# Where the third down product is added, which quarter of weights starts the groups of seven, and which engine rounds the sums of the weights

## The reference, cut to what matters

```python
x = x + tanh(g_ffn[0]) * ffn(layernorm(x))
# ffn: x is (2048, 256); Wg, Wu are (8, 256, 1024), Wd is (8, 1024, 256)
for wg, wu, wd in zip(Wg, Wu, Wd):
    h = silu(x @ wg) * (x @ wu)
    acc = acc + h @ wd
```

## Time and profile before

| | |
|---|---|
| median of 3 runs | 1277.64 us (1277.58 to 1279.3) |
| profiled execution: time, span of its instructions | 1277.64 us, 1275.6 us |
| PE busy (matmuls) | 1242.6 us, 97% |
| PEld busy | 987.7 us, 77% |
| DVE busy | 1105.9 us, 87% |
| POOL busy | 968.8 us, 76% |
| ACT busy | 691.4 us, 54% |
| granted TensorE clock | 0.995 |
| mean DMA rate | 38 GB/s |

### The profile page before, as it was taken

One profiled execution on the slowest core, in us unless ns is written; L12 is line 12 of the kernel. 1 busy time (PEld: TensorE's weight loads), 2 busy tenths in 40 slices (PEclk: granted clock), 3 DMA queues, 4 the chain that ended last, 5 costly groups with the idle time before them and its releaser, 6 DMA issues.

```text
span 1275.6 us, 18422 instructions
## 1 busy us (share of the span) xinstructions
PE 1242.6 (97%) x6149; PEld 987.7 (77%) x6149; DVE 1105.9 (87%) x1779; ACT 691.4 (54%) x1456; POOL 968.8 (76%) x901
## 2 busy tenths in 40 slices
PE   7999999999999999999999999999999999999998
PEld 5778777777777777777777777777777777787775
DVE  5987799999999999999999999999999974677546
ACT  2455455555555555555555555555555545545543
POOL 3635898899989999888998888899989725444435
PEclk9999999999999999999999999999999999999999
DMA  4020200001100000000000000001100330000121
GB/s 136 26 91 1 92 25 26 25 26 41 34 26 25 25 26 25 25 26 25 25 26 25 26 26 25 25 25 39 37 25 1 116 116 1 18 22 14 35 96 62
DMA packets 42365, 48.27 MB, mean 38 GB/s; under 512 B 4239, under 2 KB 40143, under 8 KB 42015
## 3 DMA queue, kind: packets, MB, share of 16 engines
q1 hardware_dynamic: 38720, 43.07, 10.3%
q0 software_dynamic: 1440, 3.41, 0.7%
q10 hardware_dynamic: 2111, 0.63, 0.2%
HBM read 37.36 MB, written 10.29 MB: 37 GB/s over the span
## 4 chain that ended last, share of the span: by engine, by line
PE 66%; DVE 17%; ACT 9%; issue 5%; POOL 2%; DMA 0%; ACTq 0%; POOLq 0%; DVEq 0%
PE bank L1270 18%; PE bank L1271 17%; PE bank L1272 17%; DVE hid_lo L1929 4%; DVE acc L1958 3%; ACT PC L1013 2%; PE bank L1508 2%; PE bank L1517 2%; DVE m_accM L1958 1%; DVE t_loT L1929 1%; ACT hid_hi L953 1%; DVE half_g L1894 1%; ACT half_g L929 1%; PE bank L1670 1%; DVE hid L1904 1%
## 5 line engine op out<-in xcount | busy, mean ns | idle before, releaser
L1270 PE MATMUL bank<-xop_hi,w_hi 128*128 128x512 f32 x896 | 352.4, 393 | 3.3 <-ACT half_g L929 2.3
L1271 PE MATMUL bank<-xop_lo,w_hi 128*128 128x512 f32 x896 | 351.8, 393 | 0.0
L1272 PE MATMUL bank<-xop_hi,w_lo 128*128 128x512 f32 x896 | 351.3, 392 | 0.0
L1921 DVE TENSOR_TENSOR hid_lo<-hid,hid_hi 128x512 fp32r<-128x512 f32 x227 | 261.0, 1182 | 3.8 <-ACT hid_hi L953 3.7
L1270 PEld LDWEIGHTS bank<-xop_hi,w_hi 128*128 128x128 f32 x896 | 168.4, 188 | 45.2 <-ACT half_g L929 3.0
L1272 PEld LDWEIGHTS bank<-xop_hi,w_lo 128*128 128x128 f32 x896 | 168.3, 188 | 38.2
L1271 PEld LDWEIGHTS bank<-xop_lo,w_hi 128*128 128x128 f32 x896 | 168.5, 188 | 37.9
L953 ACT CAST hid_hi<-hid 128x512 fp32r<-128x512 f32 x227 | 140.1, 621 | 62.3 <-PE bank L1272 48.3
L937 ACT ACTIVATE s<-bank 128x512 f32<-128x512 f32 x128 | 78.3, 612 | 109.2 <-PE bank L1272 109.2
L1270 PE MATMUL bank<-hid_hi,wd_hi 128*128 128x512 f32 x338 | 134.4, 398 | 1.4 <-DVE hid_lo L1921 1.4
L1271 PE MATMUL bank<-hid_lo,wd_hi 128*128 128x512 f32 x338 | 133.9, 396 | 0.0
(11 more groups left out here) (272 smaller groups left out, 2648.5 us busy)
## 6 DMA issues: line engine op xcount, KB each, us to landing
raw_gu<-in_L_ffn_Wg_dram SPq DMA_DIRECT2D x32, 256.0 KB, 2.7
raw_gu<-in_L_ffn_Wu_dram SPq DMA_DIRECT2D x32, 256.0 KB, 3.1
raw_d<-in_L_ffn_Wd_dram SPq DMA_DIRECT2D x32, 256.0 KB, 3.6
slots<-empty_row SPq DMA_DIRECT2D x1, 2080.0 KB, 10.0
xr<-slots SPq DMA_DIRECT2D x8, 260.0 KB, 4.8
x_res<-in_x_dram SPq DMA_DIRECT2D x4, 512.0 KB, 5.2
x_mid<-x_res SPq DMA_DIRECT2D x1, 2048.0 KB, 9.0
x_res<-x_mid SPq DMA_DIRECT2D x4, 512.0 KB, 5.6
```

Source lines behind the costliest of these rows:

```text
L1270: mm(ps, w, a, start=start, stop=False, skip_group_check=True)
L1271: mm(ps, w, a_low, start=False, stop=False, skip_group_check=True)
L1272: return mm(ps, w_low, a, start=False, stop=True, skip_group_check=True)
L1921: nc.vector.tensor_tensor(out=hid_lo[n % 2][h][:], in0=hid[h][:], in1=hid_hi[n % 2][h][:].bitcast(F32), op=ALU.subtract).then_inc(lo_ready ...
```

## The change

1. `FIRST_SEVEN = 3`: the groups of seven begin with quarter 3, not 2, so there are 28. The conditions of SP's loads and of the first `split_down_sums` move with it.
2. `group_behind_seven` adds M2 before it multiplies h11 (`hid_psum`), not after.
3. For each quarter that follows a group of seven, the casts of the down weights' sums (`wds_hi`) and of the gate and up weights' sums (W_S1 to W_S4 of `w_hi`) are ACT's (`round_down_sums`, `round_sums`); POOL posts the sums on one semaphore and waits for the casts on another. On POOL the subtraction for `wds_lo` moves behind `split_hi`, and that of the 1024 columns W_S1 to W_S4 becomes the last of `split_lo`.

```diff
+    FIRST_SEVEN = 3
         def seven(n):
-            return inside(n) and pair(n) == 0 and 2 <= quarter(n) <= NQ - 2
+            return inside(n) and pair(n) == 0 and FIRST_SEVEN <= quarter(n) <= NQ - 2
+        def rounded_by_act(q):
+            return seven(PAIRS * (q - 1))
+        def act_rounds(q):
+            return 2 * sum(rounded_by_act(i) for i in range(q))
...
-                if q >= 4:
-                    sp.wait_ge(wds_ready, q - 3)
+                if q >= FIRST_SEVEN + 2:
+                    sp.wait_ge(wds_ready, q - FIRST_SEVEN - 1)
...            split_hi(q)
-                own_step(nc.gpsimd.tensor_tensor(out=s[:, :, W_S4], in0=r[:, :, 1, f0], in1=s[:, :, W_S2], op=ALU.subtract))
-                own_wait()
-                own_step(nc.gpsimd.tensor_copy(hi[:, :, W_S1:W_S4 + 1], s[:, :, W_S1:W_S4 + 1]))
+                last = nc.gpsimd.tensor_tensor(out=s[:, :, W_S4], in0=r[:, :, 1, f0], in1=s[:, :, W_S2], op=ALU.subtract)
+                if rounded_by_act(q):
+                    last.then_inc(w_sums_ready, 1)
+                else: (as before)
...            split_lo(q)
-                nc.gpsimd.tensor_tensor(out=lo[:, :, W_S1:W_S4 + 1], ...)
+                if rounded_by_act(q):
+                    split_down_sums_lo(q - 1)
                 nc.gpsimd.tensor_tensor(out=lo[:, :, W_11:W_22], ...)
                 nc.gpsimd.tensor_tensor(out=lo[:, :, W_22], ...)
+                if rounded_by_act(q):
+                    pool.wait_ge(w_round_ready, W_ROUND + act_rounds(q) + 2)
+                nc.gpsimd.tensor_tensor(out=lo[:, :, W_S1:W_S4 + 1], ...).then_inc(gu_ready, 1)
...            split_down_sums(q)
-                own_step(nc.gpsimd.tensor_copy(wds_hi[:], wds_raw[:]))
-                own_wait()
+            def split_down_sums_lo(q):
+                pool.wait_ge(w_round_ready, W_ROUND + act_rounds(q + 1) + 1)
                 nc.gpsimd.tensor_tensor(out=wds_lo[:], in0=wds_raw[:], in1=wds_hi[:].bitcast(F32),
                                         op=ALU.subtract).then_inc(wds_ready, 1)
...            ACT's loop over n
                 fork(n, "u")
+                if n % PAIRS == 0:
+                    round_down_sums(n // PAIRS + 1)
...
                 silu_sum(n, "22", half22, sum22)
                 silu_sum(n, "12", half12, sum12)
+                if n % PAIRS == 0:
+                    round_sums(n // PAIRS + 1)
                 silu_psum(n, "21", s21, bank[FORK_BANK["g"]], p4_ps)
...            DVE, group_behind_seven(n)
                 sum_12(n, "g")
+                add_seven(n - 1, "M2")
                 hid_psum(n, "11", bank[SUM_BANK["u"]], s11, p2_ps)
-                add_seven(n - 1, "M2")
                 sum_22(n, "u")
```

More of the change, by code:

```diff
@@ L357, in flamingo_kernel @@
         joined, JOINED = x_lo_ready[1], 7
+        w_sums_ready, W_SUMS = x_sum_ready[1], 4
+        w_round_ready, W_ROUND = x_hi_ready[1], 7
         p1_ps, p2_ps, p3_ps, p4_ps, p5_ps, p6_ps, p7_ps = (
@@ L577, in split_hi @@
                 own_step(nc.gpsimd.tensor_tensor(out=s[:, :, W_S2], in0=s[:, :, W_S1], in1=r[:, :, 0, f0], op=ALU.subtract))
-                nc.gpsimd.tensor_copy(hi[:, :, W_22], r[:, :, 1, f1])
                 own_wait()
-                own_step(nc.gpsimd.tensor_tensor(out=s[:, :, W_S4], in0=r[:, :, 1, f0], in1=s[:, :, W_S2], op=ALU.subtract))
-                own_wait()
-                own_step(nc.gpsimd.tensor_copy(hi[:, :, W_S1:W_S4 + 1], s[:, :, W_S1:W_S4 + 1]))
+                own_step(nc.gpsimd.tensor_copy(hi[:, :, W_22], r[:, :, 1, f1]))
+                last = nc.gpsimd.tensor_tensor(out=s[:, :, W_S4], in0=r[:, :, 1, f0], in1=s[:, :, W_S2], op=ALU.subtract)
+                if rounded_by_act(q):
+                    last.then_inc(w_sums_ready, 1)
+                else:
+                    own_step(last)
+                    own_wait()
+                    own_step(nc.gpsimd.tensor_copy(hi[:, :, W_S1:W_S4 + 1], s[:, :, W_S1:W_S4 + 1]))
             def split_lo(q):
@@ L589, in split_lo @@
                 own_wait()
-                nc.gpsimd.tensor_tensor(out=lo[:, :, W_S1:W_S4 + 1], in0=s[:, :, W_S1:W_S4 + 1],
-                                        in1=hi[:, :, W_S1:W_S4 + 1].bitcast(F32), op=ALU.subtract)
+                if rounded_by_act(q):
+                    split_down_sums_lo(q - 1)
                 nc.gpsimd.tensor_tensor(out=lo[:, :, W_11:W_22], in0=r[:, :, :, f0],
@@ L594, in split_lo @@
                 nc.gpsimd.tensor_tensor(out=lo[:, :, W_22], in0=r[:, :, 1, f1], in1=hi[:, :, W_22].bitcast(F32),
-                                        op=ALU.subtract).then_inc(gu_ready, 1)
+                                        op=ALU.subtract)
+                if rounded_by_act(q):
+                    pool.wait_ge(w_round_ready, W_ROUND + act_rounds(q) + 2)
+                nc.gpsimd.tensor_tensor(out=lo[:, :, W_S1:W_S4 + 1], in0=s[:, :, W_S1:W_S4 + 1],
+                                        in1=hi[:, :, W_S1:W_S4 + 1].bitcast(F32), op=ALU.subtract).then_inc(gu_ready, 1)
             def split_down(q):
@@ L613, in split_down_sums @@
                 f0, f1 = slice(0, P), slice(P, 2 * P)
-                if q == 2:
+                if q == FIRST_SEVEN:
                     pool.wait_ge(x_kept, X_KEPT + 16)
@@ L622, in split_down_sums @@
                 own_wait()
-                own_step(nc.gpsimd.tensor_tensor(out=wds_raw[:, S4], in0=d[:, 1, f0], in1=wds_raw[:, S2], op=ALU.subtract))
-                own_wait()
-                own_step(nc.gpsimd.tensor_copy(wds_hi[:], wds_raw[:]))
-                own_wait()
+                nc.gpsimd.tensor_tensor(out=wds_raw[:, S4], in0=d[:, 1, f0], in1=wds_raw[:, S2],
+                                        op=ALU.subtract).then_inc(w_sums_ready, 1)
+            def split_down_sums_lo(q):
+                pool.wait_ge(w_round_ready, W_ROUND + act_rounds(q + 1) + 1)
                 nc.gpsimd.tensor_tensor(out=wds_lo[:], in0=wds_raw[:], in1=wds_hi[:].bitcast(F32),
@@ L960, in t_hi_part, with round_down_sums, round_sums @@
                 nc.scalar.copy(t_hi[i][:], t_raw[i][:]).then_inc(t_hi_ready, 1)
+            def round_down_sums(q):
+                if not rounded_by_act(q):
+                    return
+                act.wait_ge(w_sums_ready, W_SUMS + act_rounds(q) + 1)
+                nc.scalar.copy(wds_hi[:], wds_raw[:]).then_inc(w_round_ready, 1)
+            def round_sums(q):
+                if not rounded_by_act(q):
+                    return
+                act.wait_ge(w_sums_ready, W_SUMS + act_rounds(q) + 2)
+                nc.scalar.copy(w_hi[q % 2][:, :, W_S1:W_S4 + 1, :], w_raw[q % 2][:, :, W_S1:W_S4 + 1, :]).then_inc(w_round_ready, 1)
             for n in range(GROUPS + 1):
```

## The result

The changed kernel takes **1258.25 us** (median of 4, 1256.19 to 1260.54) against 1277.61 for the one before (1277.38 to 1279.3): ratio 0.985 (95% interval 0.983 to 0.988). 1263.5 was forecast. The profiled execution took 1260.54 us, with a span of 1258.8 and a granted clock of 0.995, the same clock as in the profiled execution of before.

A forecast was written before the change was run, and what follows sets the result against it. PE was taken to bound the feed-forward stage, losing time between matmul starts. 1277.64 - 11.6 (waits at M5) - 3.2 (first group of seven) + 0.7 (extra matmuls) = 1263.5 us; range for 8 in 10: 1260.5 to 1273.

The forecast's parts named there:

- The 0.40 of M5: At M5 in each group of seven, PE's wait and slow restart cost 0.40 us, 11.6 us over 29 groups.
- a few hundredths: Elsewhere in the feed-forward stage, no other repeating place was found that costs more than a few hundredths of a us.
- (d): Rival: M5's stall moves elsewhere, such as an ACT copy held by the new wait for POOL; 1268 to 1276 us; chance 0.08.
- M5's 0.30: At M5, the wait of 0.30 us is covered by M2's addition coming 0.60 us earlier.
- DVE comes earlier by what that first sum comes earlier: In DVE's chain from POOL's first hidden sum to `sum_22(g)`, the sum's lead carries through: 1.1 us, or 0.7 at the bound.
- 3.2 for the opening: At the first group of seven, three PE idle times and restarts, caused by late POOL, cost 3.2 us and should go.
- 0.7 back: On PE, one group more has eight down products: 3 matmuls at 0.23, +0.7 us.
- the 0.86 for faster: Chance of a measurement faster by more than 2.6 us, counting the forecast, (a), (b) and most of (d).
- (a): Rival: POOL's shift brings DVE nothing, the wait at product4 u stays at 0.32 us; 1272.2 us; chance 0.17.
- (b): Rival: the stall at the first group of seven returns one quarter later, the rest holds; 1266.7 us; chance 0.08.
- (c): Rival: POOL's long subtraction starts too late and holds both h multiplications; slower from about 414.3; 1282.5 us; chance 0.09.
- its price for the experiment: For the new subtraction order without ACT's casts: M5's distance 0.9 us instead of 0.53, 29 x 0.37 = 10.7 us slower.

The follow-up runs named there:

- the cast one step later: Changed kernel with ACT's cast of the 1024 gate and up sum columns moved behind silu of block 21: 1260.0 us, ratio 0.986.
- part 3 alone: Kernel before with ACT's casts and POOL's new subtraction order; groups of seven still from quarter 2, M2 still behind h11: 1258.68 us, ratio 0.986.
- the cast two steps later: Changed kernel with ACT's cast of the 1024 gate and up sum columns moved behind the cast of h22: 1279.14 us, ratio 1.001.
- part 2 alone: Kernel before with only M2 added before h11 is multiplied: 1277.34 us, ratio 1.000.

## Why the prediction was right, and where not

**The steps that failed.** 14.1 us were forecast and 19.4 measured, 17.1 between the two profiled executions. What made the sum too small are two terms that it put at nothing: the small distances of a quarter (1.9 us) and the new order in quarters 0 and 1 (about 1.0). And the lower end of the range left out that an execution can lack the stretch at half the clock, which took the median 2.3 us further down. In the mechanism one step is wrong: DVE's chain does not come earlier by all that the first hidden sum comes earlier. Each is taken up below.

**What bounds the kernel: right.** PE bounds the stage, M5's wait was the loss that repeats, and the distance between starts, not PEld's 20.9 us, measures it.

**The size for each quarter: too small.** 0.40 was forecast and 0.47 measured. The 0.40 of M5 is all gone. The other 0.07 was written off as "a few hundredths": M1's second matmul came 0.251 behind the first and now comes 0.234, M7's 0.247 and now 0.229, and there are several of 2 to 8 ns. Over 27 quarters this is 1.9 us.

**Part 1: right,** 2.9 expected and 3.7 measured by itself. Of the 0.8 beyond the sum, 0.4 is the wait at M5 that quarter 3 does not have either. Beside part 3 it does something that I had not worked out: it keeps ACT's new wait for POOL away from the one quarter in which POOL is late, which costs PE 2.1 us at one place. The forecast named the mechanism as (d), but thought of it in all quarters and not in the opening.

**Part 2: right that it is worth little by itself,** 0.09 a quarter forecast and 0 measured. It is also worth nothing beside part 3, which the text had not said; 0.6 us of head start do nothing where DVE is earlier by more than M5's 0.30.

**Part 3: right in its effect, with one step that does not hold.** The last subtraction was to start 0.44 behind `sum_22(u)` (413.05 - 412.61), and it starts 0.31 behind (405.25 - 404.94), released by ACT's cast, as forecast. The cast takes 1.03, not 1.09. The first hidden sum was to come 0.7 to 1.1 us earlier and comes 5.12 - 4.05 = 1.07 earlier. What reaches `sum_22(g)` is less: 13.71 and now 13.00, 0.71. "DVE comes earlier by what that first sum comes earlier" is the sentence that does not hold: the experiment with the cast one step later made 2.04 us at the first sum into 0.42. Here the difference did no harm, since 0.71 is more than M5 and product4 u need; it did harm in that experiment's expectation, which rested on the same sentence.

**The time up to the M4 of quarter 3: a term was missing.** 4.2 us measured, 3.3 in the sum: 3.2 for the opening, 0.7 back, and 0.8 for the waits at M5 of quarters 2 and 3, which both lie ahead of that M4. The edit's effect in quarters 0 and 1 was not costed at all; the diff moves the long subtraction for every quarter, and I read it for those behind a group of seven only. That is the 0.9: 0.97 us of lead are there at 73.63, before any group of seven, and by itself this edit made 1.5 us.

**The range: too narrow at the lower end.** 1258.25 lies under 1260.5. From the profiled execution the sum misses 1260.54 by 3.0: 1.9 in the quarters, 0.9 ahead of them, and 0.2 in the tail and outside the span. Like with like the result would thus have stood at the very edge of the range. The other 2.3 us of the median are the half clock, which the profiled execution has and two of the result's four have not (1256.2 and 1256.3 at a clock of 1.000), so that the median lies between the groups. The profile of before has it too: the busy time of 61.5 to 68.3 us stands there at a PEclk of 0.50. I had read the clock of the stage, 1.00, and not that of the time ahead of it. A stretch that one execution has and another may not have belongs to both ends of a range. The 0.2% of the measurement (2.6 us) was given as a bound of what counts as a change and not added below. The chances do not add up as told, either: the 0.86 for faster takes in 0.03 of the 0.08 of (d), not most of it.

**The rivals.** (a) is out: DVE came earlier by enough. (b) is out. (c) was not reached: the subtraction started at 0.31 behind `sum_22(u)`, which is 412.92 in its terms, against its 414.1. With the order alone, which meets its condition, the kernel is slower, as it says; but it set the loss at product4 u, its price for the experiment (10.7 us, 11.3 measured) was taken at M5, and the loss is at M1. That the price agrees is luck. (d) is real in one quarter of part 3 alone, and in each quarter of the kernel with the cast two steps later.

## What to carry to other kernels

Where two engines hand over whole instructions, ask which instruction is running when the critical one is issued, and put a short one or none there. POOL's lighter load is not what gave the gain: with one of its two casts given back the time is the same, and what counts is that its longest instruction began 1.59 us ahead of DVE's two multiplications, and the first hidden sum 1.07 us earlier. With the same order and both casts on POOL it began 0.09 ahead of them, and the kernel was 11.3 us slower than before. Follow a delay through the turns one by one, since a turn that changes places can swallow most of it. And read an edit for the loops' first rounds as well: there it met another stage and gave 1 to 1.5 of the 17 us.

## What the runs showed of the hardware

- A DVE `tensor_scalar` of 128x4, f32 from SBUF to SBUF, takes 0.17 us alone and up to 1.83 us when it is issued inside a GpSimd subtraction of 1024 columns; it ends when that does. The Trainium skill ("SBUF — State Buffer", section "Who interferes with whom") lists `tensor_scalar` among the instructions that can take the shared ports; the trace agrees, for an instruction of 4 columns.
- A PE wait of some tenths costs more than its own length: the second matmul behind it comes 0.34 us later instead of 0.23, at M5 before, at product4 u with part 2 alone; behind the waits of the cast two steps later it is 0.31 at M1 and 0.34 at product4 u. With the cast one step later the second matmul of product4 u comes 0.32 us behind the first although the first is on time.
- A stretch of 6.8 us at half the clock (PEclk 0.50, 18 matmuls in place of 32) comes and goes between executions of one program, with the engine busy throughout it. It costs about 2.7 us.
